# Router stages rank nodes by running counts and two matmuls per group; biases of the node and output layers are added by VectorE

## The chip, the cores and the metric
One core of a Trainium2 chip. The metric is the device time of one execution of the whole program, in microseconds (us): 5182.44 us before, the median of three runs (5175.28 to 5185.94).

## The reference, cut to what matters
A graph of 6250 nodes with 256 features and 106,250 edges goes through two layers, and every part adds to x:

```
x += gcn(layernorm(x))        # relu(A @ (h W1) + b1), then A @ (h W2) + b2
x += moe(layernorm(x))        # 6 experts, top 2 by a small router network
x += gnn(layernorm(x))        # x1 = mish(h Wd + bd); agg = sum relu(x1[src] + mish(edge We + be))
                              # out = mish((x1 + agg) Wo + bo)
x += moe(layernorm(x))        # 8 experts, top 2 by a linear router
```
mish(z) = z tanh(softplus(z)). The biases that the change touches are b2 (of the first part), bd (dense) and bo (out). All arithmetic is float32.

## The kernel before, in words
Nodes stand in tiles of 128 (a node per partition) and are worked on in groups of up to four tiles (UNITS: twelve groups of four tiles and a last one of one tile). x stays in SBUF for the whole program. Stages run one after the other, each with its own buffers and semaphores, and between two of them stands a barrier of all engines. Within a stage the order of the work on each engine is written out by hand; there is no planner. Every `chain(...)` and `link(...)` on VectorE waits for the instruction just issued.

The stages in order: setup; support (h W1, lines 302 to 378); convolution over the edges; hidden; convolution again; router 0 with the dispatch to its experts (stage_dispatch, mix 0); experts 0; nodes (stage_nodes: the weighted outputs of the experts are added to x, then x1); edges; router 1 (stage_dispatch, mix 1); experts 1; the last additions. The change touches support, router 0, nodes and router 1.

Support, a loop over 13 groups in halves of two tiles. VectorE: normalise (line 281) four tiles, copy (342) two halves from PSUM; ScalarE copies transposes; TensorE transposes and multiplies; SyncE stores rows. VectorE does the normalisation of group g+1 before the copies of group g.

Router stages, for group u. TensorE: turned (transposes, 931), hidden (1357, router 0 only), ranks (1380 to 1384) of the group before, logits (1365 or 1370), product (1341, then 1342 for the bias) of a later group: two ahead in router 0, three ahead in router 1, which has two PSUM buffers for it. Product waits until VectorE has taken the earlier product (`moments_ready`). The bias is the sum of three bf16 rows, multiplied by ones of three partitions; `split_bias` (866 to 873) makes these rows by ten linked VectorE instructions at the start of the stage, behind which `parts_ready` releases TensorE and ScalarE. VectorE: added (1487, or 1491 and 1492), moments (897, 900), biased (1503), chose (1514 to 1529: the two best experts of a node as a mask `chosen`), refined (913 to 917), rows_of (1536 to 1545: the row to which a node goes for each of its two experts), bounded (1480, router 1 only: min(z, 20), the start of mish). ScalarE: evacuated, factor (the four activations of mish, router 1), guessed, spread (923: the normalised nodes), rectified (1434, router 0). GpSimd scatters the nodes to the experts' rows, two indirect DMAs for each tile, when `row_ready` says so.

In ranks each node gets the number of nodes ahead of it that chose the same expert: one matmul of the strict upper triangle `before` by `chosen`, one of all ones by the tiles 1, 2 and 3 back (three matmuls of 24, 16 and 8 columns), and four of all ones for the group's total.

Nodes stage, for group u. VectorE: combined(u+1) (998 and the moments), finished(u-1) (1019), refined(u+1), bounded(u) (1011). ScalarE: evacuated, factor(u-1), guessed and spread of u+1, keep(u-2). TensorE: turned(u), turned_back(u-2), product(u) (1104, with 1105 for the bias). GpSimd gathers the experts' outputs.

Of the kernel before, what the change touches and what calls it, by code (L numbers as in the profile page):

```python
# [9 lines left out]
ALU = mybir.AluOpType  # L10
# [3 lines left out]
P = 128  # L14
# [6 lines left out]
TG = 4  # L21
# [279 lines left out]
def stage_support(nc, c):  # L301

    io = c.io
    with ExitStack() as ctx:
# [7 lines left out]
        rows = [sb(f"s_rows{h}", [P, 2, HID]) for h in range(2)]  # L312
        ps_t = [pb(f"s_pt{h}", [P, KD, 2 * P]) for h in range(2)]
        ps_y = [pb(f"s_py{h}", [P, 2, HID]) for h in range(2)]
        w_in, own = sem("s_w_in"), sem("s_own")
# [6 lines left out]
        @block.sync  # L322
        def _(sp):
            sp.dma_start(w1[:], io["g_w1"]).then_inc(w_in, 16)
            with sp.Fori(0, G) as g:
                for h in range(2):
                    store_rows(sp, c.t1, g, h, rows, rows_ready, rows_out)

            for h in range(2):
                sp.wait_ge(rows_out[h], 16)  # L330

        @block.vector
        def _(dve):
# [3 lines left out]
            def copy_rows():  # L337
                for h in range(2):
# [5 lines left out]
                    dve.sem_inc(rows_ready[h], 1)  # L344

            for h in range(2):
                dve.sem_inc(py_free[h], 1)
                normalise(dve, nc, c, xn[h], 0, h, xn_ready[h])
            with dve.Fori(0, G - 1) as g:
# [4 lines left out]
                copy_rows()  # L354
            copy_rows()
# [579 lines left out]
def stage_nodes(nc, c):  # L935
# [5 lines left out]
    with ExitStack() as ctx:  # L941
# [5 lines left out]
        bias, parts, ones = bias_buffers(sb)  # L947
# [6 lines left out]
        w_in, parts_ready, own, act_own, parts_own = sem("w_in"), sem("parts_ready"), sem("own"), sem("act_own"), sem("parts_own")  # L954
# [22 lines left out]
        def _(sp):  # L977
            sp.dma_start(wd[:], io["l_wd"]).then_inc(w_in, 16)
            sp.dma_start(bias[0][:], io["l_bd"]).then_inc(w_in, 16)
# [8 lines left out]
        def _(dve):  # L988
# [33 lines left out]
            nc.vector.memset(ln2[:], LN2)  # L1022
            nc.vector.memset(ones[:], 1.0)
# [17 lines left out]
        def _(act):  # L1041
# [31 lines left out]
            act.wait_ge(parts_ready, 1)  # L1073
# [17 lines left out]
        def _(pe):  # L1091
# [6 lines left out]
            def product(u):  # L1098
# [3 lines left out]
                for s in range(UNITS[u][1]):  # L1102
                    for k in range(KD):
                        pe.matmul(ps_y[u % 2][:, s, :], xt[:, k, s * P:(s + 1) * P], wd[:, k, :], start=k == 0, stop=False)
                    last = pe.matmul(ps_y[u % 2][:, s, :], ones[:], parts[:], start=False, stop=True)
# [8 lines left out]
            pe.wait_ge(parts_ready, 1)  # L1114
# [137 lines left out]
def stage_dispatch(nc, c, mix):  # L1252
# [8 lines left out]
    with ExitStack() as ctx:  # L1261
# [4 lines left out]
        bias, parts, ones3 = bias_buffers(sb)  # L1266
        if mix == 0:
# [3 lines left out]
            loads = [(wx[:, 0, :], "g_w2"), (bias[0][:], "g_b2"), (w1[:], "r0_w1"), (b1[:], "r0_b1"), (w2[:], "r0_w2")]  # L1271
        else:
            wx = sb("wx", [P, KD, D])
            gamma, beta, w2 = sb("gamma", [P, KD]), sb("beta", [P, KD]), sb("w2", [P, KD, E1])
            q, ln2 = pair(sb, "q", [P, TG, D]), sb("ln2", [P, 1])
            loads = [(wx[:], "l_wo"), (bias[0][:], "l_bo"), (gamma[:], "r1_gamma"), (beta[:], "r1_beta"), (w2[:], "r1_w2")]
# [8 lines left out]
        is_nth, chosen = sb("is_nth", [P, 2, NT, 8]), pair(sb, "chosen", [P, TG, 8])  # L1285
        first, running = sb("first", [P, 8]), pair(sb, "running", [P, 8])
# [12 lines left out]
        w_in, parts_ready = sem("w_in"), sem("parts_ready")  # L1299
        own, act_own, parts_own = sem("own"), sem("act_own"), sem("parts_own")  # L1300
# [4 lines left out]
        logit_ready, exp_ready, chosen_ready = sem("logit_ready"), sem("exp_ready"), sem("chosen_ready")  # L1305
# [28 lines left out]
        def _(pe):  # L1334
            def product(u):
# [3 lines left out]
                for s in range(n):  # L1339
                    for k in range(mix + 1):  # L1340
                        pe.matmul(ps_x[u % X][:, s, :], c.feat[:, k, (t + s) * P:(t + s + 1) * P], wx[:, k, :], start=k == 0, stop=False)
                    last = pe.matmul(ps_x[u % X][:, s, :], ones3[:], parts[:], start=False, stop=True)
# [30 lines left out]
            def ranks(u):  # L1373
                n = UNITS[u][1]
                flat = lambda ap: ap.rearrange("p t e -> p (t e)")
                now = chosen[u % 2]
                pe.wait_ge(chosen_ready, u + 1)
# [328 lines left out]
```

## Time and profile before

| | |
|---|---|
| median of three runs | 5182.44 us |
| the profiled execution's own time | 5180.41 us |
| its span | 5178.6 us |
| TensorE busy | 3895.7 us (75%) |
| VectorE busy | 1965.5 us (38%) |
| ScalarE busy | 1566.8 us (30%) |
| GpSimd busy | 2875.4 us (56%) |

The share of busy time is a mean over stages with different limits. The four stages of the change fill about 690 us of the span: support from 73 to 129 us, router 0 from 2398 to 2642, nodes from 3019 to 3187, router 1 from 4313 to 4540. The row "PEclk" of the page gives the clock that was granted to TensorE, in tenths of 2.4 GHz: 9 in support, 5 to 6 in the slices of router 0 and of router 1, 7 to 9 in the other stages.

### The profile page before, as it was taken

The page shows a single profiled execution, that of the slowest core. Times are in us where ns is not written, and L with a number is a line of the kernel's source. Part 1 is how long each engine was busy: PE and PEld are TensorE (multiplying, and loading weights), DVE is VectorE, ACT ScalarE, POOL GpSimd, SP SyncE. Part 2 cuts the span into 40 slices and gives each one's busy share as a digit, 9 for nine tenths or more (in the row PEclk, how much of TensorE's full clock was granted, in tenths as well). Part 3 has the DMA queues.
Part 4 walks back from the last instruction along what each step waited for, and adds up shares of the span by engine and source line. Part 5 has one row for each costly group of instructions (what it writes and reads, how often), then busy time and mean ns, then how long its engine had stood idle before and what let it go on. Part 6 is the DMA issues. An engine that isn't in the chain of part 4 may idle for free. (4 is left out here: it accounts for less than half of the span.)

```text
span 5178.6 us, 61257 instructions
## 1 busy us (share of the span) xinstructions
PE 3895.7 (75%) x16707; PEld 3012.1 (58%) x16707; DVE 1965.5 (38%) x4145; ACT 1566.8 (30%) x1876; POOL 2875.4 (56%) x2950
## 2 busy tenths in 40 slices
PE   3688888885788898896959966666666667769980
PEld 2455555553556565564548755666666665558870
DVE  4344344433344444433423354333333334511113
ACT  1344444443344444443201145212122123411110
POOL 0677777772777777772420055777777772600007
PEclk9778788876787778776579976555555556689995
DMA  3455555554454554552132234666666662242214
GB/s 95 140 175 171 166 173 173 177 169 116 125 156 150 157 157 150 155 156 69 66 130 85 81 113 133 197 200 197 201 199 199 200 198 61 82 154 65 65 61 144
DMA packets 336091, 733.21 MB, mean 142 GB/s; under 512 B 67797, under 2 KB 184672, under 8 KB 335897
## 3 DMA queue, kind: packets, MB, share of 16 engines
q1 hardware_dynamic: 160968, 392.16, 21.9%
q0 software_dynamic: 118176, 284.72, 20.1%
q10 hardware_dynamic: 56880, 55.58, 3.2%
q8 instruction: 25, 0.41, 0.0%
q14 instruction: 42, 0.34, 0.0%
HBM read 521.27 MB, written 210.91 MB: 141 GB/s over the span
## 5 line engine op out<-in xcount | busy, mean ns | idle before, releaser
L582 PE MATMUL conv_pz<-conv_we,conv_edge 128*128 128x256 f32 x3360 | 1221.0, 498 | 0.0
L1188 PE MATMUL x_pa<-x_hot,x_node 128*128 128x64 f32 x3360 | 765.7, 423 | 359.6 <-PEq L72 359.6
L464 POOL DMA_INDIRECT conv_gath<-support_table,conv_idx x840 | 808.0, 962 | 404.1 <-issue 249.8
L1173 POOL DMA_INDIRECT x_node<-node_table,x_idx x840 | 852.3, 1015 | 297.2 <-issue 234.9
L464 POOL DMA_INDIRECT conv_gath<-hidden_table,conv_idx x840 | 808.8, 963 | 346.7 <-issue 247.4
L1188 PEld LDWEIGHTS x_pa<-x_hot,x_node 128*128 128x128 f32 x3360 | 732.5, 331 | 393.0 <-issue 393.0
L582 PEld LDWEIGHTS conv_pz<-conv_we,conv_edge 128*128 128x128 f32 x3360 | 729.3, 241 | 181.7 <-issue 49.5
L573 PE MATMUL conv_ps<-conv_hot,conv_gath 128*128 128x64 f32 x3360 | 524.5, 311 | 358.9 <-DMA conv_gath<-support_table,conv_idx 187.7
L573 PEld LDWEIGHTS conv_ps<-conv_hot,conv_gath 128*128 128x128 f32 x3360 | 474.0, 221 | 404.5 <-DMA conv_gath<-support_table,conv_idx 197.3
L883 ACT ACTIVATE conv_q<-conv_q 128x1024 f32<-128x1024 f32 x210 | 221.9, 1057 | 1201.2 <-ACTq L72 1176.9
L1209 DVE TENSOR_TENSOR x_node<-x_node,x_neg 128x1024 f32<-128x1024 f32 x210 | 257.4, 1226 | 626.4 <-DMA x_node<-node_table,x_idx 626.4
L1198 ACT ACTIVATE x_node<-x_node 128x1024 f32<-128x1024 f32 x210 | 221.9, 1057 | 899.2 <-ACTq L72 899.2
L474 DVE TENSOR_SCALAR conv_q<-conv_pz 128x1024 f32<-128x1024 f32 x210 | 257.2, 1225 | 608.8 <-DVEq L72 606.9
L675 POOL DMA_INDIRECT cb_outs<-expert_outs,row x98 | 96.0, 980 | 523.1 <-PEq L658 493.6
L782 PE MATMUL e_ph<-e_xt,e_w_first 128*128 128x256 f32 x1376 | 313.6, 385 | 61.6 <-PEq L72 61.6
L1326 POOL DMA_INDIRECT expert_rows<-r_xn,r_row x196 | 196.8, 1004 | 291.3 <-DVE r_row L1545 238.3
L821 ACT ACTIVATE e_hid<-e_ph,e_b_first 128x256 f32<-128x256 f32 x344 | 137.8, 473 | 710.4 <-ACTq L72 710.4
L490 DVE TENSOR_TENSOR sums_table<-sums_table,conv_ps 128x64 f32 x420 | 93.3, 222 | 618.0 <-DVEq L72 615.5
L782 PEld LDWEIGHTS e_ph<-e_xt,e_w_first 128*128 128x128 f32 x1376 | 259.7, 192 | 106.1 <-issue 73.1
L971 POOL DMA_INDIRECT n_outs<-expert_outs,row x98 | 95.1, 970 | 400.6 <-POOLq L97 367.4
L583 PEld LDWEIGHTS conv_pz<-conv_bias_parts,conv_ones 3*128 3x128 bf16 x840 | 77.8, 93 | 365.0 <-issue 365.0
L583 PE MATMUL conv_pz<-conv_bias_parts,conv_ones 3*128 3x256 bf16 x840 | 258.8, 308 | 0.0
(221 smaller groups left out, 4234.4 us busy)
## 6 DMA issues: line engine op xcount, KB each, us to landing
conv_edge<-in_edge_t SPq DMA_DIRECT2D x210, 512.0 KB, 5.0
edge_mish_table<-conv_neg SPq DMA_DIRECT2D x210, 512.0 KB, 3.1
x_neg<-edge_mish_table SPq DMA_DIRECT2D x210, 512.0 KB, 3.5
e_rows<-expert_rows SPq DMA_DIRECT2D x114, 256.0 KB, 3.0
expert_outs<-e_outs ACTq DMA_DIRECT2D x114, 256.0 KB, 2.2
expert_outs<-conv_zeros ACTq DMA_DIRECT2D x35, 512.0 KB
conv_gath<-support_table,conv_idx POOLq DMA_INDIRECT x840
conv_gath<-hidden_table,conv_idx POOLq DMA_INDIRECT x840
```

Of the source, the lines that this page charges most:

```text
L464: pool.indirect_dma_start(gath[s][:, j, :], None, table[:, :], bass.IndirectOffsetOnAxis(ap=idx[:, half, col:col + 1], axis=0),).then_inc( ...
L474: nc.vector.tensor_scalar(q[r][:], ps_z[r][:], ZMAX, None, ALU.min).then_inc(z_ready[r], 1)
L573: last = pe.matmul(ps[s % 2][:], gath[s][:, j, :], hot[half][:, at + j, :], start=j == 0, stop=j == CG - 1)
L582: pe.matmul(ps_z[r][:, j, :], edge[r][:, m, j * P:(j + 1) * P], we[:, m, :], start=m == 0, stop=False)
L583: last = pe.matmul(ps_z[r][:, j, :], ones[:], parts[:], start=False, stop=True)
L782: last = pe.matmul(out[:, m, :], w[:, k, m * P:(m + 1) * P], given[:, k, :], start=k == 0, stop=k == KD - 1)
L883: link(act, act.activation(q, q, ACT.Exp), own)
L1173: pool.indirect_dma_start(node[s][:, j, :], None, c.t3[:, :], bass.IndirectOffsetOnAxis(ap=idx[:, half, col:col + 1], axis=0),).then_inc(g ...
L1188: last = pe.matmul(ps_a[n][:, m, :], node[s][:, j, m * P:(m + 1) * P], hot[n][:, j, :], start=j == 0, stop=j == CG - 1)
L1198: act.activation(node[s][:], node[s][:], ACT.Relu, scale=-1.0).then_inc(msg_ready, 1)
L1209: nc.vector.tensor_tensor(node[s][:], node[s][:], neg[s % RING][:], ALU.add).then_inc(own, 1)
L1326: pool.indirect_dma_start(c.rows_d[:, :], bass.IndirectOffsetOnAxis(ap=row[0:rows, t + s, k:k + 1], axis=0), xn[u % RING][0:rows, s, :], None,
```

## The change
1. Routers: `split_bias`, its buffers and its semaphore go. The constants are made ahead of the wait for the loads, with `consts_ready` in place of `parts_ready`.
2. Router 0: product no longer adds b2; the load of b2 leaves this stage.
3. Support: b2 is loaded for all partitions, VectorE waits for it before its first instruction, and after each copy it adds b2 to the two tiles of x that have been normalised.
4. Nodes and router 1: the bias is loaded for all 128 partitions; product has no matmul for it; bounded first adds it to the product in PSUM (128x1024 elements), waits, and then takes the minimum.
5. Routers, ranks: VectorE multiplies `chosen` by a table of ones and zeros (`upto`) and sums, which gives for each tile the count of the tiles ahead of it in the group and, as a fifth, the total. TensorE then needs two matmuls: ones by these sums (40 columns) and `before` by `chosen` (32 columns), into the same PSUM. The convolution stages keep their three bf16 rows.

```diff
@@ support, VectorE
                     dve.sem_inc(rows_ready[h], 1)
+                    half = c.x[:, bass.ds(g * TG + 2 * h, 2), :]
+                    nc.vector.tensor_tensor(half, half, b2[:].unsqueeze(1).to_broadcast([P, 2, D]), ALU.add)
+            dve.wait_ge(b_in, 16)
             for h in range(2):
@@ nodes, bounded (router 1 has the same with ps_x)
                 dve.wait_ge(py_ready, u + 1)
+                chain(nc.vector.tensor_tensor(ps_y[u % 2][:, 0:n, :], ps_y[u % 2][:, 0:n, :], bias[:].unsqueeze(1).to_broadcast([P, n, D]), ALU.add))
                 nc.vector.tensor_scalar(q[u % 2][:, 0:n, :], ps_y[u % 2][:, 0:n, :], ZMAX, None, ALU.min).then_inc(z_ready, 1)
@@ nodes and routers, start of VectorE's work
             dve.wait_ge(w_in, 32)
-            split_bias(dve, nc, c, bias, parts, parts_own)
-            dve.sem_inc(parts_ready, 2)
@@ routers, product on TensorE
                     for k in range(mix + 1):
-                        pe.matmul(ps_x[u % X][:, s, :], c.feat[...], wx[:, k, :], start=k == 0, stop=False)
-                    last = pe.matmul(ps_x[u % X][:, s, :], ones3[:], parts[:], start=False, stop=True)
+                        last = pe.matmul(ps_x[u % X][:, s, :], c.feat[...], wx[:, k, :], start=k == 0, stop=k == mix)
@@ routers, ranks on TensorE
-                pe.matmul(flat(ps_r[:, 0:n, :]), before[:], flat(now[:, 0:n, :]), start=True, stop=n == 1)
-                for d in range(1, n):
-                    pe.matmul(flat(ps_r[:, d:n, :]), ones[:], flat(now[:, 0:n - d, :]), start=False, stop=d == n - 1)
-                for s in range(n):
-                    last = pe.matmul(ps_r[:, TG, :], ones[:], now[:, s, :], start=s == 0, stop=s == n - 1)
-                last.then_inc(rank_ready, 1)
+                pe.matmul(flat(ps_r[:, 0:n + 1, :]), ones[:], flat(sums[u % 2][:, 0:n + 1, :]), start=True, stop=False)
+                pe.matmul(flat(ps_r[:, 0:n, :]), before[:], flat(chosen[u % 2][:, 0:n, :]), start=False, stop=True).then_inc(rank_ready, 1)
@@ routers, end of chose on VectorE
-                last.then_inc(chosen_ready, 1)
+                chain(last)
+                slots = upto[:, 0:n + 1, :, 0:n]
+                taken = now.rearrange("p s e -> p e s").unsqueeze(1).to_broadcast([P, n + 1, 8, n])
+                chain(nc.vector.tensor_tensor(counted[:, 0:n + 1, :, 0:n], taken, slots, ALU.mult))
+                nc.vector.tensor_reduce(sums[u % 2][:, 0:n + 1, :], counted[:, 0:n + 1, :, 0:n], AX.X, ALU.add).then_inc(sums_ready, 1)
```

## Rows read from the trace of the kernel before

**Rows 1.** Busy time by engine, granted clock and DMA in steady stretches of both routers
```profile
2434.00:2582.00 148.00, 137.32 (x440) 83.58 (x439) 62.76 (x360) 39.46 (x81) 65.29 (x68) 0.56 0.17 60
4377.00:4480.00 103.00, 95.59 (x464) 69.83 (x464) 68.04 (x297) 62.01 (x90) 62.40 (x59) 0.75 0.22 77
```
**Rows 2.** Timeline, router 0's start: start us, us, engine, line [idle before, its releaser]
```profile
2404.17 0.28 DVE L866 CAST r_bias_high<-r_bias 3x256 bf16<-3x256 f32 x1 [5.09 <-DMA r_before<-in_before]
...
2409.46 1.19 PE L1341 MATMUL r_px<-r_wx,sums_table 128*128 128x256 f32 x2 [22.66 <-DVEq L1555]
...
2410.59 0.39 PE L1342 MATMUL r_px<-r_bias_parts,r_ones 3*128 3x256 bf16 x1
...
2410.91 1.22 PE L1341 MATMUL r_px<-r_wx,sums_table 128*128 128x256 f32 x2
```
**Rows 3.** Timeline, router 0's loop
```profile
2437.86 1.22 DVE L1487 TENSOR_TENSOR x_sb<-x_sb,r_px 128x1024 f32<-128x1024 f32 x1 [4.15 <-PE r_px L1342]
...
2487.54 1.22 DVE L1487 TENSOR_TENSOR x_sb<-x_sb,r_px 128x1024 f32<-128x1024 f32 x1 [5.18 <-PE r_px L1342]
...
2505.03 1.22 DVE L1487 TENSOR_TENSOR x_sb<-x_sb,r_px 128x1024 f32<-128x1024 f32 x1 [5.18 <-PE r_px L1342]
...
2519.53 1.22 DVE L1487 TENSOR_TENSOR x_sb<-x_sb,r_px 128x1024 f32<-128x1024 f32 x1 [3.80 <-PE r_px L1342]
...
2582.49 1.22 DVE L1487 TENSOR_TENSOR x_sb<-x_sb,r_px 128x1024 f32<-128x1024 f32 x1 [5.18 <-PE r_px L1342]
...
2588.04 0.16 DVE L917 SCALAR_TENSOR_TENSOR r_shift<-mv,rstd 128x4 f32<-128x4 f32 x1
...
2590.93 1.66 PE L1365 MATMUL r_pl<-r_w,r_hid 128*128 128x6 f32 x8 [1.60 <-ACT r_hid L1434]
```
**Rows 4.** Timeline, router 0's last but one ranks
```profile
2606.76 0.63 PE L1380 MATMUL r_pr<-r_chosen,r_before 128*128 128x32 f32 x2 [0.37 <-DVE r_chosen L1526]
...
2608.49 1.85 PE L1384 MATMUL r_pr<-r_chosen,r_ones 128*128 128x8 f32 x8
```
**Rows 5.** Lines 1543 and 1608: ns min/median/max, first and last start us, forms
```profile
L1543 DVE TENSOR_REDUCE r_row_f<-r_picked x52: 151/178/187, 2447.0 to 4512.9; 128x4 f32<-128x32 f32 x48, 128x1 f32<-128x8 f32 x4
...
L1608 DVE TENSOR_TENSOR r_picked<-r_is_nth,r_start_f x4: 558/562/569, 2620.1 to 4517.0; 128x392 f32<-128x392 f32 x4
```
**Rows 6.** Timeline, support's loop on VectorE
```profile
104.76 0.42 DVE L342 COPY s_rows<-s_py 128x256 f32<-128x256 f32 x1 [0.55 <-DVEq L72]
...
106.21 1.39 DVE L281 TENSOR_SCALAR s_xn<-x_sb,mv,rstd 128x256 f32 x4 [1.02 <-DVEq L72]
```
**Rows 7.** Line 281: VectorE's register instructions for an address in x
```profile
L281 DVEq FUSED_REGOPS  x96: 65/84/117, 77.4 to 121.9; - x96
```
**Rows 8.** Line 859: a VectorE add of two tiles
```profile
L859 DVE TENSOR_TENSOR e_outs<-e_py,e_b_last x114: 691/691/693, 2677.0 to 5036.9; 128x512 f32<-128x512 f32 x114
```
**Rows 9.** Timeline, support's start
```profile
73.71 0.36 SPq L324 DMA_DIRECT2D gw<-in_g_w  x1
74.46 1.38 DVE L281 TENSOR_SCALAR s_xn<-x_sb,mv,rstd 128x256 f32<-128x256 f32 x4 [1.41 <-PEq L97]
...
76.07 1.94 PE L290 MATMUL s_pt<-ident_sb,s_xn 128*128 128x128 f32 x8 [76.07 <-PEq L72]
```
**Rows 10.** Timeline, router 1's loop
```profile
4432.73 1.23 DVE L1480 TENSOR_SCALAR r_q<-r_px 128x1024 f32<-128x1024 f32 x1 [3.53 <-PE r_px L1342]
...
4438.26 2.08 PE L1341 MATMUL r_px<-r_wx,messages_table 128*128 128x256 f32 x4 [1.04 <-DVE mv L900]
...
4446.40 1.22 DVE L1480 TENSOR_SCALAR r_q<-r_px 128x1024 f32<-128x1024 f32 x1 [3.53 <-PE r_px L1342]
...
4481.06 0.96 POOL L1326 DMA_INDIRECT expert_rows<-r_xn,r_row  x1 [2.91 <-DVE r_row L1545]
```
**Rows 11.** Timeline, nodes' first combined and the finished with the least idle before it
```profile
3031.58 3.38 DVE L998 SCALAR_TENSOR_TENSOR x_sb<-n_outs,gate,x_sb 128x256 f32<-128x256 f32 x8 [4.18 <-DMA n_outs<-expert_outs,row]
...
3115.19 1.22 DVE L1019 SCALAR_TENSOR_TENSOR n_rows<-n_q,n_py 128x1024 f32<-128x1024 f32 x1 [1.83 <-ACT n_q L1066]
```

More of the change, by code:

```diff
@@ L946, in stage_nodes @@
         wd = sb("wd", [P, KD, D])
-        bias, parts, ones = bias_buffers(sb)
+        bias = sb("bias", [P, D])
         ln2 = sb("ln2", [P, 1])
@@ L978, in _ @@
             sp.dma_start(wd[:], io["l_wd"]).then_inc(w_in, 16)
-            sp.dma_start(bias[0][:], io["l_bd"]).then_inc(w_in, 16)
+            sp.dma_start(bias[:], io["l_bd"]).then_inc(w_in, 16)
             for u, (t, n) in enumerate(UNITS):
@@ L1103, in product @@
                     for k in range(KD):
-                        pe.matmul(ps_y[u % 2][:, s, :], xt[:, k, s * P:(s + 1) * P], wd[:, k, :], start=k == 0, stop=False)
-                    last = pe.matmul(ps_y[u % 2][:, s, :], ones[:], parts[:], start=False, stop=True)
+                        last = pe.matmul(ps_y[u % 2][:, s, :], xt[:, k, s * P:(s + 1) * P], wd[:, k, :], start=k == 0, stop=k == KD - 1)
                 last.then_inc(py_ready, 1)
@@ L1270, in stage_dispatch @@
             hid = sb("hid", [P, GN])
-            loads = [(wx[:, 0, :], "g_w2"), (bias[0][:], "g_b2"), (w1[:], "r0_w1"), (b1[:], "r0_b1"), (w2[:], "r0_w2")]
+            loads = [(wx[:, 0, :], "g_w2"), (w1[:], "r0_w1"), (b1[:], "r0_b1"), (w2[:], "r0_w2")]
         else:
@@ L1340, in product @@
                     for k in range(mix + 1):
-                        pe.matmul(ps_x[u % X][:, s, :], c.feat[:, k, (t + s) * P:(t + s + 1) * P], wx[:, k, :], start=k == 0, stop=False)
-                    last = pe.matmul(ps_x[u % X][:, s, :], ones3[:], parts[:], start=False, stop=True)
+                        last = pe.matmul(ps_x[u % X][:, s, :], c.feat[:, k, (t + s) * P:(t + s + 1) * P], wx[:, k, :], start=k == 0, stop=k == mix)
                 last.then_inc(px_ready, 1)
@@ L1478, in bounded @@
                 n = UNITS[u][1]
+                got = ps_x[u % X][:, 0:n, :]
                 dve.wait_ge(px_ready, u + 1)
+                chain(nc.vector.tensor_tensor(got, got, bias[:].unsqueeze(1).to_broadcast([P, n, D]), ALU.add))
                 nc.vector.tensor_scalar(q[u % 2][:, 0:n, :], ps_x[u % X][:, 0:n, :], ZMAX, None, ALU.min).then_inc(z_ready, 1)
@@ L1548, in _ @@
                 nc.vector.memset(logit[r][:], -1e30)
-            nc.vector.memset(ones[:], 1.0)
-            nc.vector.memset(ones3[:], 1.0)
+            chain(nc.vector.memset(upto[:], 0.0))
+            for s in range(1, TG + 1):
+                nc.vector.memset(upto[:, s, :, 0:s], 1.0)
             if mix == 1:
                 nc.vector.memset(ln2[:], LN2)
+            nc.vector.memset(ones[:], 1.0).then_inc(consts_ready, 1)
             dve.wait_ge(w_in, 16 * len(loads))
-            split_bias(dve, nc, c, bias, parts, parts_own)
-            dve.sem_inc(parts_ready, 2)
             nc.vector.tensor_scalar(first[:], iota8[:], float(REGION), None, ALU.mult)
@@ L1697 @@
         "g_w2": a["L0_gnn_W2"],
-        "g_b2": np.broadcast_to(a["L0_gnn_b2"], (3, D)),
+        "g_b2": np.broadcast_to(a["L0_gnn_b2"], (P, D)),
     }
```

44 lines of the change are left out of this document (22 added, 22 removed).

## The prediction
> **What bounds the kernel now.** The shares of the page say little here: the change touches four stages of twelve, so I read each of them by itself. In each, the first view is the timeline around its first instructions (what releases the stage), the second the timeline of two or three rounds of its loop (which wait comes back each time), the third the busy times with the granted clock.
>
> Router 0: at its start VectorE has waited for the last load and then runs the ten linked instructions of the split, and TensorE's first product waits behind them, from 2404.17 to 2409.46 [rows 2]. In its loop every VectorE addition (line 1487) waits for the product, 4 to 5 us each time [rows 3], and TensorE is busy 137 of 148 us at 0.56 of full clock [rows 1]: TensorE closes the round. But a second chain is nearly as long: from the addition over VectorE's moments, chose and refined, ScalarE's spread and rectified, to the logits. Where TensorE is a little ahead, it waits for that chain: 1.60 us before the logits at 2590.93 [rows 3].
>
> Router 1: one serial round of 13.67 us (4432.73 to 4446.40): VectorE's bounded, added and moments take 5.5 us to the start of the product at 4438.26, the product 8.1 us to the next bounded [rows 10]. GpSimd, which ends the stage, still waits for rows at 4481.06 (idle 2.91) [rows 10] and hardly afterwards.
>
> Support: VectorE's own queue is the round. Nothing else is waited for; the gaps of 0.55 and 1.02 us are its semaphore and register instructions [rows 6]. Nodes: ScalarE and TensorE close the round; VectorE has at least 1.83 us of idle before finished, but for the first group [rows 11].
>
> **The change, part by part.** Minus is a gain.
>
> *Router 0.* (a) Start: the split goes, 2409.46 - 2404.17 = 5.3 us, all of it ahead of TensorE; the load of b2 goes too, one DMA issue on SyncE ahead of the last load, by the 0.36 us of one issue [rows 9]. Together -5.6. What is late next is the last load itself. (b) Product: from the bias matmul to the next tile are 2410.91 - 2410.59 = 0.32 us, and a tile takes 2410.91 - 2409.46 = 1.45 [rows 2]. Four tiles save 1.28 us at this clock (1.2 GHz). Three rounds at the start have no ranks in them: -3.8. (c) The loop proper: nine rounds from 2437.86 to 2582.49, 144.6 us; a slow one is 17.49 (2487.54 to 2505.03), a fast one 14.50 (to 2519.53) [rows 3]. Ranks at half clock take 2606.76 to 2608.49 + 1.85 = 3.6 us for 16 record pairs of ones and `before` [rows 4]; two matmuls (four pairs) leave about a quarter, 0.9 to 1.1. So TensorE's chain shortens by 1.3 + 2.6 us in a slow round and the other chain closes it. That one grows: chose gets two instructions and two waits. Their price lies between 0.18 us (32 elements) and 0.56 (392 elements) [rows 5]; for 160 elements I take 0.30 each, nearer the lower row, plus the overlap lost to the waits: 0.66 in all (ends 0.4 and 1.2). The new slow round: addition to refined 2588.04 - 2582.49 = 5.55, plus 0.66, then 2.89 to the logits (2590.93), 1.5 logits, product 4 x (1.45 - 0.32) = 4.5, 0.1 to the addition: 15.2 to 15.3 us. The fast round, with logits of 0.9 and part of the product at full clock, comes to 14.1 to 14.2. Of the nine rounds four are slow, one is between: 4 x 2.2 + 1 + 4 x 0.4 = -11 (ends: all slow -7, all fast -17). (d) The last round, with a product of one tile, is closed by the other chain already: +0.35. The last ranks that GpSimd waits for come 1.3 sooner. Router 0: -5.6 - 3.8 - 11 + 0.35 - 1.3 = **-21.4** (-17 to -27). GpSimd has idle before nearly every group, so it isn't late next.
>
> *Support.* The extra instruction is an addition of two tiles; the nearest row is 0.69 us [rows 8], and its address needs one or two register instructions of 0.08 each (some 0.12 apart) [rows 7]. VectorE's queue runs ahead of the engine, so some of it lies beside the semaphore instructions. Between the two copies stand five of them in 0.55 us, 0.11 each [rows 6]: three come before the addition, two beside it. The second copy comes at 0.33 + 0.25 + 0.69 - 0.08 = 1.19 instead of 0.55: +0.63. The second addition starts 0.58 after its copy and ends at 1.27; the loop's own instructions behind it (0.7 to 0.8 of the 1.02) reach the next normalisation at 1.35: +0.33. Per group +0.95; twelve loop rounds and one first half at the end: +12.0. The very last addition lies beside the store. VectorE's new wait at the start: the load before it is usable 76.07 - 73.71 = 2.36 us after its issue, the new one one issue later, so the first normalisation moves from 74.46 to about 76.4; TensorE did nothing before 76.07 anyway and starts at 77.2 to 77.4 [rows 9]: +1.3, and what is queued behind that wait is the whole of VectorE's work. Support: **+13.3** (+3 if only the register instructions show, +26 with all 26 additions, 0.94 each, in full and 1.9 at the start).
>
> *Nodes.* Start: the split lies beside the first gather, for which VectorE still waits 4.18 us [rows 11]: 0. Loop: bounded gets an addition of 128x1024, 1.22 us as line 1487 [rows 3], and its wait: +1.24 a group on VectorE. Behind it are combined and finished; finished has 1.83 us of cover at the least [rows 11], so 0.6 remains and the round stays; the product's gain is hidden too, since bounded starts behind refined. The first group has no cover, but its product ends 1.3 us sooner. In the last two groups ScalarE stands close behind bounded: +0.75 and +0.45. Nodes: **+1.2** (0 to +8).
>
> *Router 1.* Start as in router 0, without the missing load: -5.2; the load of the bias is now 128 rows, within 0.2. The round: +1.24 for the addition, which nothing covers, as product waits for the moments; the product loses four bias matmuls, three at 0.32 and one, at full clock, some 0.2: -1.17. Net +0.08, ten rounds +0.8. chose and the shorter ranks lie in VectorE's 3.5 us of idle and in TensorE's 1.04 [rows 10]: 0. The rows of the group at 4481.06 come behind one more addition: +1.24. Router 1: **-3.2** (-9 to +7, by the clock of the product).
>
> A rule of the Trainium skill speaks against this part ("TensorE: Matmul & The Clock Gate", the Part on the clock gate): TensorE's default is the throttled clock, and activity releases it. Work is taken from TensorE here, so by it the product could stay at 1.2 GHz.
>
> **Sum.** -21.4 + 13.3 + 1.2 - 3.2 = -10.1 us. The profiled execution took 5180.41 us (span 5178.6), 2.0 below the median of the three runs, so 5170.3 by the profile and 5172.3 beside the median. I say **5172**.
>
> **The rivals.** (1) The clock falls. The row for it: in router 0 the clock is at 0.56 although TensorE is busy 93% [rows 1], so it is low with little idle already, and idle comes on top. Against it: router 1, busy 93% as well, has 0.75 [rows 1], so the busy share alone doesn't set it. Price: router 1's product wholly at 1.2 GHz is 4 x 2.0 = 8.0, with 6.8 of VectorE 14.9 instead of 13.67, +12 over ten rounds; router 0 all slow +4: 5188. By the page's rule this is where it would go. (2) VectorE's additions cost less and router 0's rounds all take 14.2: -6 more there, and -6 in support, if the additions lie beside more of its queue: 5160. For it: every slow round of before has the long ranks in it. (3) The slower side: the addition is exposed wherever it stands. It decides in nodes: once finished's cover of 1.83 is used up (a turn of TensorE at full clock shortens the round by some 0.7), each of 13 groups costs 1.24, +15 over my sum, and support +12.7 more, at the full 0.94: 5200. Against it: most groups have 2 to 3 us there. (4) The routers' starts don't gain, since something else releases TensorE there: +10, 5182. Against it: the release is named as line 1555, right behind the split [rows 2].
>
> **How the numbers follow.** 0.2% of this kernel, 10.4 us, is about what a measurement can tell from no change. The forecast 0.50, of which half lies beyond -10.4 (own range 5163 to 5181); rival 1 0.13; rival 2 0.22; rival 3 0.07; rival 4 0.05; something else 0.03. Faster by over 0.2%: 0.25 + 0.22 + 0.02 = 0.49; within: 0.25 + 0.13 + 0.05 + 0.01 = 0.44; slower: 0.07. The range leaves out rival 3 and the far ends of support's and router 0's bounds: 5157 to 5187.
>
> **What would show it.** Router 0's first product about 0.1 us behind the last load's landing; line 1487 coming every 14.1 to 15.3 us, TensorE waiting for r_hid before line 1365 in every round; support's rounds 0.95 us longer, the second copy 1.2 us behind the first instead of 0.55; line 1480 still every 13.6 to 13.8 us in router 1 with about 6.8 us from the bias addition to the product; nodes unchanged within 2 us. I am wrong if support's round grows by less than 0.5 or over 1.3 us, if router 1's round moves by more than 0.5, or if router 0 as a whole gains less than 15 us.

## The result, and the profile after

| | before | after |
|---|---|---|
| median of five runs each | 5175.87 us (5175.28 to 5185.94) | 5153.29 us (5151.17 to 5159.08) |
| ratio, 95% interval | | 0.9953 (0.9939 to 0.9968) |
| span of the profiled execution | 5178.6 us | 5151.5 us |

The kernel is 0.47% faster, by more than the 0.2% that a measurement can tell. Forecast were 5172 us and -10.1 us. Stage by stage, each from its first instruction to the next stage's first, in us:

| | before | after | measured | forecast |
|---|---|---|---|---|
| support | 56.15 | 64.79 | +8.6 | +13.3 |
| hidden (not touched) | 42.14 | 43.65 | +1.5 | 0 |
| router 0 | 243.81 | 219.29 | -24.5 | -21.4 |
| nodes | 167.82 | 169.72 | +1.9 | +1.2 |
| router 1 | 226.67 | 216.53 | -10.1 | -3.2 |
| the other stages | | | -4.5 | 0 |

The stages add up to the difference of the two profiled spans, 27.1 us; the medians differ by 22.6. Of the profiles used further down, those of c2, e3, e5 and e11 are of executions over 1.5% slower than the fastest of their kernel.

The busy times by engine in both routers' loops after, as in [rows 1]: the columns are the stretch, its length, busy us of PE, PEld, DVE, ACT and POOL, granted clock, DMA share and GB/s.
```profile
2434.47:2566.42 131.95, 84.01 (x290) 61.54 (x289) 67.47 (x379) 39.47 (x81) 66.25 (x70) 0.73 0.19 68
4324.34:4443.14 118.80, 85.75 (x394) 72.47 (x393) 95.75 (x380) 74.11 (x108) 61.72 (x60) 0.76 0.19 66
```
TensorE's clock in router 0 has risen from 0.56 [rows 1] to 0.73, though TensorE is now busy only 84 of 132 us. I had set out the opposite as a rival. In router 1 it is 0.76, against 0.73 in the nine rounds of before (4348.89 to 4473.71).

The mean hides where the clock rose. Two stretches of one round of router 0 after, same columns: hidden, then the logits with the product.
```profile
2481.21:2483.19 1.98, 1.98 (x4) 0.67 (x4) 1.81 (x21) 0.50 (x2) 0.84 (x1) 1.00 0.37 132
2487.76:2493.04 5.28, 5.28 (x17) 4.46 (x17) 0.55 (x3) 0.22 (x1) 3.98 (x5) 0.50 0.30 104
```
Hidden had 0.50 in the same place of a slow round before (2490.50 to 2494.28). Over the loops its records fell from 1088 to 618 ns on average, while those of the logits, which come behind a wait, rose from 309 to 361 ns, and nearly every product has 0.50.

Timeline after, router 0: the start, and one round of the loop (for [rows 2, 3]).
```profile
2411.02 3.78 PE L1343 MATMUL r_px<-r_wx,sums_table 128*128 128x256 f32 x8 [16.94 <-DMA r_before<-in_before]
...
2478.58 1.22 DVE L1485 TENSOR_TENSOR x_sb<-x_sb,r_px 128x1024 f32<-128x1024 f32 x1 [3.00 <-PE r_px L1343]
...
2483.39 0.42 DVE L1531 TENSOR_TENSOR r_counted<-r_chosen,r_upto 128x160 f32<-128x160 f32 x1
2483.84 0.32 DVE L1532 TENSOR_REDUCE r_sums<-r_counted 128x40 f32<-128x160 f32 x1
...
2484.86 0.16 DVE L922 SCALAR_TENSOR_TENSOR r_shift<-mv,rstd 128x4 f32<-128x4 f32 x1
...
2487.76 1.87 PE L1366 MATMUL r_pl<-r_w,r_hid 128*128 128x6 f32 x8 [2.91 <-ACT r_hid L1430]
2489.49 3.76 PE L1343 MATMUL r_px<-r_wx,sums_table 128*128 128x256 f32 x8
...
2493.28 1.22 DVE L1485 TENSOR_TENSOR x_sb<-x_sb,r_px 128x1024 f32<-128x1024 f32 x1 [3.00 <-PE r_px L1343]
```
The product now waits for the last load itself. (Each matmul stands in the trace as records: two for one in f32, one in bf16.) In the loop TensorE waits for r_hid each round, and the round is 14.70 us: 6.28 to L922, 2.90 to the logits, 1.73, and 3.79 for the product. Each of the nine rounds takes 14.4 to 14.7 us.

Router 1 before, where my price for the bias matmul came out wrong: two tiles of the product that begins at 4438.26 [rows 10].
```profile
4440.26 0.39 PE L1342 MATMUL r_px<-r_bias_parts,r_ones 3*128 3x256 bf16 x1
...
4440.58 2.08 PE L1341 MATMUL r_px<-r_wx,messages_table 128*128 128x256 f32 x4
...
4442.59 0.39 PE L1342 MATMUL r_px<-r_bias_parts,r_ones 3*128 3x256 bf16 x1
...
4442.91 1.97 PE L1341 MATMUL r_px<-r_wx,messages_table 128*128 128x256 f32 x4
```
Router 1 after, one round:
```profile
4416.16 1.23 DVE L1477 TENSOR_TENSOR r_px<-r_px,r_bias 128x1024 f32<-128x1024 f32 x1 [1.76 <-PE r_px L1343]
4417.43 1.22 DVE L1478 TENSOR_SCALAR r_q<-r_px 128x1024 f32<-128x1024 f32 x1
...
4422.95 6.61 PE L1343 MATMUL r_px<-r_wx,messages_table 128*128 128x256 f32 x16 [2.46 <-DVE mv L905]
...
4429.60 1.23 DVE L1477 TENSOR_TENSOR r_px<-r_px,r_bias 128x1024 f32<-128x1024 f32 x1 [1.97 <-PE r_px L1343]
```
A tile with its bias took 4442.91 - 4440.58 = 2.33 us at 1.2 GHz. With no bias between them the records stand 0.427 apart at that clock (start times of the single records), so a tile of four without bias is 1.71, and the bias costs 0.62, not 0.32. Of the 0.62, 0.21 is a record half as long as the others; 0.14 passes before it starts and the rest behind it. Router 1's round is 13.44 here, 6.79 of it VectorE and 6.65 the product (8.14 before). Tile by tile this product lost 0.45, 0.62, 0.41 and 0.10 us: before, the clock went to full 6.38 us into it, ahead of the last tile; after, 5.88 us into it, in the middle of the last tile. The shorter product gets less of the full clock, 0.54 on average for 0.60.

Support after, one round on VectorE (for [rows 6]):
```profile
87.18 0.42 DVE L344 COPY s_rows<-s_py 128x256 f32<-128x256 f32 x1
88.04 0.69 DVE L348 TENSOR_TENSOR x_sb<-x_sb,s_b 128x512 f32 x1 [0.44 <-DVEq L72]
88.65 0.42 DVE L344 COPY s_rows<-s_py 128x256 f32<-128x256 f32 x1
89.51 0.69 DVE L348 TENSOR_TENSOR x_sb<-x_sb,s_b 128x512 f32 x1 [0.44 <-DVEq L72]
90.24 1.40 DVE L281 TENSOR_SCALAR s_xn<-x_sb,mv,rstd 128x256 f32 x4
91.55 0.42 DVE L344 COPY s_rows<-s_py 128x256 f32<-128x256 f32 x1
```

### The profile page after: what moved, and what is told of

Read it like the earlier page. It is cut to its first block and busy times, and to the rows that moved or that the text cites. A ratio compares the mean times of both kernels' runs of the same rounds, so it can differ in the third digit from the quotient of the medians.

```text
span 5151.5 us, 60460 instructions
## 1 busy us (share of the span) xinstructions
PE 3786.7 (74%) x16272; PEld 2974.7 (58%) x16272; DVE 2015.3 (39%) x4226; ACT 1568.8 (30%) x1876; POOL 2872.9 (56%) x2950
```

## The experiments

Six of these sixteen runs were timed where the convolutions take their 1115 us (e7 to e10, e15, e16). The other ten were made on three chips whose gathers are slower (e1 to e4, then e5 and e6, then e11 to e14): a convolution takes 1520 to 1650 us there and either kernel 6250 to 6480, so a whole time tells nothing of a change of 20 us. There I compare stages, with both kernels profiled once more (c1 and c2, on the chip of e5 and e6). Support agrees with the first profiles within 0.4 us, router 0 is 6 to 7 us longer and router 1 6 to 8, and one kernel's stage can differ by 5 us from profile to profile. Times are us; "round" is from one addition or minimum to the next.

| stage | before there (c1) | after there (c2) |
|---|---|---|
| support, hidden | 56.14, 42.15 | 64.44, 43.67 |
| router 0 | 250.75 | 225.19 |
| nodes | 199.40 | 207.44 |
| router 1 | 233.10 | 224.48 |

**Ranks alone, and biases alone.** Theory: the gain that I missed is the bias matmul. Rival: it is the ranks, by way of the clock. e1 is the kernel before with part 5 of the change, e2 the changed kernel without it:
```diff
-                pe.matmul(... ones[:], sums ...)     # e1 adds these two to before,
-                pe.matmul(... before[:], chosen ...) # e2 takes them from after
+                pe.matmul(flat(ps_r[:, 0:n, :]), before[:], flat(now[:, 0:n, :]), start=True, stop=n == 1)
...
+                for s in range(n):
+                    last = pe.matmul(ps_r[:, TG, :], ones[:], now[:, s, :], start=s == 0, stop=s == n - 1)
```


> The kernel before with the counts by VectorE and the two matmuls for ranks alone; all biases as before. Theory (the gain that I missed is the bias matmul, which costs 0.62 us a tile at 1.2 GHz, not the 0.32 that I took): in router 0 VectorE's chain closes the rounds at once, since the product still takes 4 x 1.47 = 5.9 us: 6.3 from the addition to refined, 2.9 to the logits, 1.6, 5.9, 0.1, so slow rounds of 16.8 instead of 17.49, fast ones as before, last ranks 1.5 sooner: router 0 -3 to -6 us; router 1's rounds stay at 13.67 us, TensorE only waits longer for the moments. In all -3 to -7 us. Rival (the short ranks let TensorE's clock rise, and that is what made both routers faster): router 0 gains 15 us or more with rounds of 14.7, router 1 gains 5 or more, in all -20.

> The changed kernel with the old ranks (up to eight matmuls per group, no counts by VectorE). Theory: router 1 stays as in the changed kernel (216.5 us, rounds of 13.2 to 13.6); in router 0 TensorE closes the slow rounds again, 17.49 - 4 x 0.62 = 15.0 us, the fast ones are 14.1, and the last ranks come 1.5 us later: router 0 some 219 to 223 us. In all 0 to +5 us to the changed kernel. Rival (ranks and clock): router 1 goes back to rounds of at least 14.3 us (13.67 + 1.24 - 4 x 0.15 or more) and router 0 to 230 us or more, in all +15 or more.

e1: router 0 251.06 (c1: 250.75; -3 to -6 was expected), its rounds mostly 16.9 as worked out; router 1's rounds 13.65 to 13.84, the stage 232.23. The ranks alone give nothing that shows: the chain with the product in it closes the rounds, at about the mean of what c1 has, 14.8 to 17.7. e2: router 0 222.49, router 1 219.84. The biases alone give all of it, within the 5 us between profiles. A second run of e2:

> The changed kernel with the old ranks once more, as the first run of it was on a chip with slow gathers. It tells what the counts and the two matmuls give in router 0 beside the biases. By rows of the changed kernel: TensorE's chain with the old ranks is 17.49 - 4 x 0.62 = 15.0 us in slow rounds, 14.0 in fast ones, against 14.7 by VectorE's chain with the counts; last ranks 1.8 us later. Router 0 219 to 223, in all 0 to +4 us to the changed kernel. Rival (the ranks carry most of router 0's gain): router 0 at 228 or more.

226.44 and 224.59, against 225.19 and 224.48 of the changed kernel in c2. By the two runs, the two matmuls and the counts that they need change router 0 by -1.3 and +2.7 us, on three different chips: no effect that can be told from nothing. The rival, a gain of 15 us by the ranks, is out.

**The price of the bias matmul: left out, twice, in other forms.** e3 leaves `pe.matmul(..., ones3[:], parts[:], ...)` out of the kernel before in nodes and routers, e4 issues it twice in the routers.

> The kernel before without the bias matmul of product in both routers and in nodes, and nothing in its place, so these biases are left out; the split is still made. It prices the bias matmul by itself. Theory (0.62 us a tile at 1.2 GHz, 0.40 at 2.4): router 1's product takes 6.0 to 6.7 us instead of 8.1 and its round 11.4 to 12.1 instead of 13.67, ten rounds -16 to -22; router 0's slow rounds fall by 2.4 to 15.0, the stage -12 to -18; nodes within 2 us. In all -28 to -40. Rival (0.32 a tile, as I predicted): router 1's round 12.5, -12, router 0 -8 to -10, in all -20.

> The kernel before with each bias matmul of the two routers issued twice (the bias counts twice there). It tells where the 0.62 us sit. Theory: most of it is what stands between an f32 matmul and the bf16 one, ahead of it (0.57 instead of 0.43 to its start) and behind it (0.59 instead of 0.43 in the next tile's first), so a second one right behind the first adds only about 0.2 us (half of the 0.43 between two f32 matmuls of as many columns) at 1.2 GHz: router 1's round 13.67 + 0.6 to 0.8 = 14.3 to 14.5, in all +12 to +18 over both routers. Rival (each three-row matmul costs its 0.62 wherever it stands): router 1's round 15.7 to 16.1, in all +45 or more.

e3: router 1's undisturbed rounds took 10.96 to 12.33 us, behind a first of 12.94; two of its twelve took 19 and 21, with idle time on VectorE that the profile puts down to no instruction of the kernel (2.59 us ahead of one logits addition), so the stage (227.36) hides the gain. Router 0 took 228.71, nodes 199.99. The eight undisturbed ones are 11.5 on average, 2.2 less than 13.67 or 0.54 a tile, at a clock between the two levels; 0.32 a tile would have left 12.4. e4: ten rounds of 14.66 on average (four of 13.2 to 13.4, six of 15.4 to 15.9, by the clock of the product), +1.0, for four more bias matmuls, 0.25 each. So the price sits around the first and not in the matmul:
```profile
5504.87 0.39 PE L1342 MATMUL r_px<-r_bias_parts,r_ones 3*128 3x256 bf16 x1
5505.06 0.42 PE L1343 MATMUL r_px<-r_bias_parts,r_ones 3*128 3x256 bf16 x1
5505.41 1.53 PE L1341 MATMUL r_px<-r_wx,messages_table 128*128 128x256 f32 x3
```
The second starts 0.19 behind the first. What makes the stall, the change of type or the change to 3 rows? e9 and e12 change the kernel before:
```diff
-  last = pe.matmul(ps_x[u % X][:, s, :], ones3[:], parts[:], start=False, stop=True)
+  last = pe.matmul(ps_x[u % X][:, s, :], ones[0:1, :], bias[0][0:1, :], start=False, stop=True)   # e9: f32, 1 row
+  last = pe.matmul(ps_x[u % X][:, s, :], ones_b[:], parts_b[:], start=False, stop=True)           # e12: bf16, 128 rows
```


> The kernel before with the bias in product as one f32 row times one f32 row of ones, instead of three bf16 rows. It tells whether the 0.4 us around the bias matmul come with the change of type. If they do, nothing stands around it and it costs its two records of 0.43: router 1's tile is 6 x 0.427 = 2.56 us at 1.2 GHz (2.33 with bf16) and its round some 14.2 to 14.6. If they come with the change from 128 rows to few, they stay: tile 2.9 to 3.0 and round 15 to 15.5. For router 0's clock: if the change of type holds it down, it rises to about 0.73 here; if more work between the waits holds it down, it stays at 0.5 to 0.6.

> The kernel before with the bias matmul of the routers on 128 bf16 rows (the three parts and 125 rows of zeros, by ones) instead of 3. It tells whether the stall around the bias matmul and the low clock come from the few rows or from the type. Rows: no stall, the tile is 1.71 + 0.21 = 1.9 us at 1.2 GHz (2.33 with 3 rows), router 1's round 12.0 to 12.6 instead of 13.67, and router 0's clock 0.68 to 0.75. Type: tile 2.3 and round 13.7 as before, clock of router 0 0.56 to 0.62.

Timeline of TensorE in router 1's product, first e9 (f32, one row), then e12 (bf16, 128 rows):
```profile
4599.11 2.05 PE L1341 MATMUL r_px<-r_wx,messages_table 128*128 128x256 f32 x4
4601.10 1.22 PE L1342 MATMUL r_px<-r_bias,r_ones 1*128 1x256 f32 x2
4602.24 1.22 PE L1341 MATMUL r_px<-r_wx,messages_table 128*128 128x256 f32 x2
```
```profile
5609.92 1.91 PE L1342 MATMUL r_px<-r_wx,messages_table 128*128 128x256 f32 x4
5611.63 0.42 PE L1343 MATMUL r_px<-r_parts_b,r_ones_b 128*128 128x256 bf16 x1
5611.84 1.85 PE L1342 MATMUL r_px<-r_wx,messages_table 128*128 128x256 f32 x4
```
With 128 rows nothing is lost: 1.71 us for the four records, 0.21 for the bias, 1.92 a tile. With one f32 row the tile is 3.14, of which 1.43 for the bias where two full records would be 0.85. So the few rows cause the stall, the type doesn't. The expected rounds of 15 to 15.5 us for e9 were far off, though: they took 21.04, because the clock stayed at 0.50 (below). Nor did e12's shorter rounds of router 1 show in the stage: nine of the twelve took 11.4 to 13.3 us, but two took 21, with VectorE idle as in e3, and the stage 233.43, as in c1. Its router 0 took 236.08, 15 less than in c1. In router 1 the gain by wide rows shows in e15 alone. The Trainium skill ("TensorEngine Tiling (Array Packing)", section Tiling Modes) says that changing the tiling mode drains TensorE. I read 3 rows beside 128 as such a change, which the page doesn't say. The traces agree with this reading: the stall is 0.41 us around the first 3-row matmul, none around a second (e4), 0.58 with one row (e9) and 0 with 128 rows (e12).

**Starts.** e8 puts one conversion in place of the ten instructions of the split.

> The kernel before with one conversion in place of the ten linked instructions of the split, so the bias rows are wrong (each holds the whole bias); product is as before. It prices the starts alone. Theory: the first product of each router comes 4.6 to 4.9 us sooner (nine tenths of 5.3), nothing else moves: router 0 and router 1 some -4.8 each, nodes 0. Rival (another release takes its place, the starts don't gain): within 1 us of before in each router. The bias matmul stays as it is, so the clock of router 0's loop stays at 0.55 to 0.62.

From the stage's start to the first product: router 0 6.11 us instead of 10.85, router 1 6.05 instead of 10.64, -4.7 and -4.6. As worked out; rival 4 is out. Router 0 as a whole took 235.58, its rounds 14.5 to 17.5 at a clock of 0.61: so much do these rounds vary by themselves (250.75 and 243.81 in the two profiles of before).

**VectorE's additions.** e5 leaves the three out of the changed kernel, e6 adds b2 elsewhere:
```diff
                 if mix == 0:
+                    chain(nc.vector.tensor_tensor(x, x, bias[:].unsqueeze(1).to_broadcast([P, n, D]), ALU.add))  # e6
                     dve.wait_ge(px_ready, u + 1)
```


> The kernel before, unchanged, once more, because the four runs before this took 1540 to 1620 us in each convolution instead of 1115, and a profile of before under the same conditions is wanted for the clock. Theory (the bias matmul between products keeps TensorE's clock low in router 0; the ranks do not): router 0's loop has a mean granted clock of 0.55 to 0.60, and the stage takes 243 to 258 us. Rival (the ranks-only kernel was slow there because short ranks let the clock fall): the rounds have at least three of 14.5 us and the stage takes 244 or less, where ranks alone took 251.

> The changed kernel, unchanged, once more beside the kernel before. All theories: support 64.8 us, router 0 219 and router 1 216.5, as these hardly depend on how fast the gathers are; the sum of the four stages some 24 us under before. Theory: clock 0.73 in router 0's loop.

> The changed kernel without VectorE's additions of b2 (support), bd (nodes) and bo (router 1), so these biases are left out; loads and waits stay. It prices the additions by stage. Theory: support's rounds go back from 4.38 to 3.72 us, 12 x 0.66 = -7.9, and the 1.9 of the start stay: 56.8 us; nodes -1 to -2; router 1's chain is VectorE then the product, so the round falls by all 1.25: 12.0 to 12.3, or less if the GpSimd queue closes it, stage -9 to -13. Rival (in router 1 the addition is half hidden, since the product is waited for anyway): router 1 -6 or less. Rival in support (the additions lie beside the register instructions and the time went at the start): support still over 60.

> The changed kernel with b2 added in router 0 instead of support: VectorE adds it to x of the group ahead of its wait for the product, where it is idle for 2.7 to 3.0 us. Support has no load, wait or addition. Theory: support back to 56.2 (-8.6), router 0 unchanged but for one load more (+0.4) and nothing in the loop, as 1.25 is less than the idle time: 219 to 220; -8 us to the changed kernel. Rival (the addition delays what stands behind it, the round grows): router 0 +6 or more, nothing gained.

c1 and c2 are the table above; router 0's clock was 0.61 in c1 and 0.72 in c2. Router 1's 224.48 is 8 over the 216.5 expected of both, its rounds the same, the rest in its last stretch. e5: support 57.64, so 6.8 us are additions and 1.5 the new wait; nodes 198.97, the 8 us more of the changed kernel on this chip gone; router 1's first rounds 10.9 to 12.7, later ones up to 16.1 (stage 217.40). e6: support 55.19 and router 0 222.33: b2 is free in router 0's wait. Hidden takes 43.64 to 43.89 in every run with additions in support and 42.13 to 42.18 without them, although nothing of it was changed. It looks like a second price of part 3, but e15 and e16, which have no additions there, took 42.9; I did not test the cause.

**What the clock follows.** e10 has TensorE compute hidden a second time, into a PSUM buffer that nobody reads, in its wait for r_hid; e13 does it from one of the 128 rows.
```diff
                 last.then_inc(ph_ready, 1)
+                for k in range(KD):
+                    pe.matmul(ps_f[:, 0:n * P], w1[:, k, :], xt[u % 2][:, k, 0:n * P], ...)              # e10
+                    pe.matmul(ps_f[:, 0:n * P], w1[0:1, k, :], xt[u % 2][0:1, k, 0:n * P], ...)          # e13
```


> The changed kernel with four more matmul records per group in router 0: hidden is computed a second time into a PSUM buffer that nobody reads, in TensorE's wait for r_hid (1.5 and 2.9 us idle per round), so the path hardly changes. It tells what made the clock of router 0's loop rise from 0.56 to 0.73. Theory A (TensorE's waits did: more f32 work in the gaps takes them away): the clock falls to 0.65 or less, and the rounds grow from 14.7 to 15.5 or more. Theory B (the bf16 matmuls between f32 ones held it down): the clock stays at 0.72 to 0.74 and the round within 0.3 us.

> The changed kernel with the same filler in router 0 as the run that computed hidden twice, but from one row of the 128: the same count and columns of matmul records, nearly nothing of the array in use. It tells what the clock follows. If it follows how much of the array works: the clock doesn't rise above 0.73, rounds stay at 14.7 or grow to 15.5, the stage 219 to 226. If it follows how much of the time TensorE is busy in the profile: 0.86 and 207 us, as with 128 rows.

Router 0's loop, same columns as above: e10, e13, e12, e1, and last router 1's loop in e9.
```profile
2428.50:2549.50 121.00, 87.11 (x328) 59.87 (x326) 68.44 (x379) 39.47 (x81) 64.35 (x67) 0.86 0.20 72
```
```profile
3477.00:3615.00 138.00, 101.47 (x331) 68.75 (x330) 68.23 (x379) 39.46 (x81) 66.45 (x70) 0.73 0.18 65
```
```profile
3405.00:3542.00 137.00, 99.08 (x430) 72.88 (x430) 61.81 (x360) 39.47 (x81) 64.50 (x68) 0.76 0.18 64
```
```profile
3368.00:3519.00 151.00, 119.67 (x326) 66.97 (x326) 68.19 (x379) 39.46 (x81) 67.20 (x71) 0.58 0.17 60
```
```profile
4486.00:4654.00 168.00, 168.00 (x512) 120.62 (x511) 70.50 (x321) 64.96 (x96) 61.62 (x64) 0.50 0.14 51
```
Both theories on e10 were wrong. More matmuls in the gaps raised the clock from 0.73 to 0.86, and router 0 fell from 219.29 to 207.11 us; here the product gains as well, its records took 541 ns instead of 646. The same number of records from one row left the clock at 0.73 (rounds 15.2 to 15.7, stage 228.13, against 0.72 and 225.19 in c2). With the bias on 128 rows and nothing else changed it was 0.76 (e12). Short ranks did nothing to it (e1, 0.58). And a TensorE that is busy without a gap, with a one-row matmul in each tile, had 0.50 throughout (e9: router 1 309.11 us, rounds of 21.04; its edges stage took 57 us more as well, for which I have no cause). So the busy share doesn't set the clock: full-height matmuls in the wait raised it, those of one row did not.

The rule of the Trainium skill that I weighed in the prediction ("TensorE: Matmul & The Clock Gate", the Part on the clock gate) is that activity releases the throttle. The traces agree for full-height matmuls (e10, 0.86) and not for those of one row (e13, 0.73); the page doesn't tell the two apart. A stage that nothing touched sets a limit to the height as well. The edges stage before:
```profile
3300.00:4200.00 900.00, 623.22 (x2737) 596.23 (x2736) 333.56 (x570) 180.67 (x171) 691.92 (x684) 0.50 0.63 199
```
All of TensorE's matmuls there have 128 rows (and 64 columns), it is busy 623 of 900 us, and it was granted 0.50 all through (so "7 to 9 in the other stages", above, leaves this stage out). Height alone doesn't account for the clock either, and what does stays open.

**Versions.** e7 is e6 with two waits shortened, e11 adds the filler:
```diff
-                    pe.wait_ge(moments_ready, u - X + 1)
+                    pe.wait_ge(px_free, u - X + 1)       # signalled right behind the last read of that PSUM buffer
...
                 if u and mix == 0:
+                    counts(u - 1)                        # behind refined(u + 1), was the end of chose(u - 1)
                     rows_of(u - 1)
```


> A version meant to beat both: b2 in router 0's wait as in the run before, and two waits shortened. In router 1 product waits until VectorE has read the PSUM buffer for the last time (the line that multiplies by it), not for the moments 3.1 us later. In router 0 the counts stand behind refined instead of ahead of it. Theory: router 1's round is VectorE up to the product plus the product, so it falls by what TensorE then waits no more, 2.4 us, from 13.43 to 11.0 to 11.5 (VectorE is busy 11.1 us a round): stage -18 to -24. Router 0's round loses the 0.75 us of the counts: 14.0 instead of 14.7, stage -5 to -7. In all -30 to -38 to the changed kernel. Rival (GpSimd's scatters, 10.2 us a round with 2.9 idle, become the bound): router 1 -5 to -10 only, with GpSimd never idle.

> The version with the two shortened waits, and in router 0 the second hidden into an unread PSUM buffer as well, since that filler took router 0 from 219.3 to 207.1 us at a clock of 0.86. Theory (full matmuls in the waits raise the clock, and the product and logits run at it): router 0's rounds 12.0 to 13.6 instead of 14.2, stage 200 to 205 instead of 211; the rest as in that version. In all 5107 to 5113 us. Rival (with the counts behind refined the chain is VectorE's and ScalarE's, and the filler only delays ranks): within 2 us of 5118.6.

e7: 5118.55 us, ratio to before 0.9896 (0.9837 to 0.9955). Router 1 200.44 with rounds of 11.5 to 12.3, router 0 211.25 with rounds of 14.2, support 55.80. e11 was timed on a chip with slower gathers: router 0 214.06 at 0.84, 11 less than in c2. But router 1 took 224.19 there, as in c2, with rounds of up to 17.75: what the early release gave in e7 didn't show. Its whole time tells nothing.

e15 is the kernel before with nothing changed but the height of every bias matmul, e16 is e11 with that in the convolutions:
```diff
-            sb("bias_parts", [3, D], BF16), sb("ones3", [3, P], BF16))
+            sb("bias_parts", [P, D], BF16), sb("ones3", [P, P], BF16))   # parts set to zero first, rows 0 to 2 as before
```


> The kernel before with every bias matmul (convolutions, nodes, both routers) on 128 bf16 rows, of which 125 are zeros, in place of 3; nothing else changed, no addition moved to VectorE. It sets the other cure beside the change's. If the few rows are the whole cost: router 1's round 11.4 to 12.5 us (stage -12 to -16), router 0 -8 to -15 with a clock of 0.70 to 0.76, and in the convolutions TensorE's busy time falls by about 0.35 us for each of 840 bias matmuls, 300 us; of that only what is not waited away for gathers shows (97.7 of 700 us are such waits), between 0 and -60 us for both. In all -25 to -85 to before. Rival (the convolutions are bound by the gathers): they stay within 3 us each and the whole gains 20 to 30.

> The version with two shortened waits, b2 in router 0's wait and the filler, and with the bias matmuls of the convolutions on 128 rows. Theory: the gains add, since the stages are apart: router 0 200 to 205 us and router 1 200 on an undisturbed chip, convolutions as in the run with wide rows everywhere. In all 5110 us less what the convolutions gain. Rival (the filler gives nothing beside the moved counts): router 0 stays at 211.

e15: 5120.67 us, ratio 0.9904 (0.9887 to 0.9920). Router 0 216.74 with the old ranks, router 1 208.33 with rounds of 11.4 and 12.6, convolutions 1106.68 and 1104.20. Router 0's loop:
```profile
2420.00:2543.40 123.40, 92.25 (x436) 66.67 (x433) 61.90 (x361) 39.48 (x81) 65.22 (x68) 0.82 0.20 72
```
So 125 rows of zeros do more than the whole change (0.9904 against 0.9953), without its 26 additions in support. Router 0 gained 27 us, where 8 to 15 were expected, at a clock of 0.82 for the expected 0.70 to 0.76. In the convolutions TensorE's saved time went into waits for gathers (176.8 us of them from 500 to 1200, 95.2 before), and 16 us came through, where I had expected up to 60. e16: 5098.73 us, ratio 0.9862 (0.9846 to 0.9879), with router 0 at 201.76 and router 1 at 199.85, as low as in any run. Its convolutions took 1112.76 and 1104.26, so of the 16 us of e15 it has 10.

## Why the prediction was wrong

- **The failed step is (b), "from the bias matmul to the next tile are 0.32 us".** It prices the record and not what it does to its neighbours: I didn't set two tiles with and without it side by side. The cost is 0.62 us at 1.2 GHz, and at full clock 1.27 - 0.87 = 0.40 (the last tile of the same product, 4445.02 to 4446.29, against four records 0.216 apart). Three tiles at the lower clock and one at the higher make 2.26 a round, where I had 1.17. By that and 1.24 for the addition, nine rounds of router 1 would have lost 9.2 us; they lost 6.0, where I had +0.8 for ten, since the shorter product gets less of the full clock (13.87 to 13.20 us on average, rounds of 11.9 to 13.6). This makes up the miss of router 1, -10.1 for -3.2, and one of my signs of being wrong came with it: its round moved by more than 0.5. In router 0 the product takes 3.79 in a slow round instead of 4.5.
- **Rival 1, the clock falls: refuted for the loops, in part true for the product.** I read the clock by how busy TensorE is. The mean of both loops rose, in router 0 from 0.56 to 0.73, and removing the few-row matmuls alone does that (e3, e12). But the rise lies in hidden, in the transposes and in waits. Behind the wait for r_hid the logits and the product run at 0.50, and in router 1 the product fell from 0.60 to 0.54, as the rival had it; at the right price of the bias that cost some 3 us and not 12.
- **Rival 2, the fastest one at 5160, lay nearest, and for another reason.** Router 0's rounds all became short, though of 14.4 to 14.7 us and not 14.2, and support came out 4.7 below the sum. But its evidence, that every slow round of before has the long ranks in it, misled: e2 and e14 have the long ranks, and at most 15.8 us.
- **Router 0's chain was right.** The three first rounds gave -5.0 us (-3.8), the nine -12.7 (-11). Addition to refined 6.28 (6.21 forecast), to the logits 2.90 (2.89), last round +0.6 (+0.35), end -1.8 (-1.3), start -5.7 (-5.6). The pair in chose cost 0.42 + 0.32 (0.30 each). But it credited the ranks with the gain in slow rounds. e1 and e2 show that the product's own saving of 2.3 us (5.88 to 3.55, from its first record to the next transpose) does that alone: it shortens both chains, the ranks only TensorE's. (The ranks of before are 16 records, eight pairs, where I wrote 16 pairs; the quarter that is left is right.)
- **Starts: right** (-5.7, -5.1; e8).
- **Support: right mechanism, term too large.** The round grew by 0.65 (4.37 for 3.72), not 0.95. The second copy came 1.05 us behind the end of the first, where 0.55 had been and 1.19 was forecast: +0.50. The next normalisation came 1.17 behind the end of the second copy, where 1.03 had been and 1.35 was forecast: +0.14. The copy stands directly behind the addition, without idle time, so VectorE's queue works off its semaphore instructions during the addition, more of them than I had taken. The start cost 1.5 (e5 against c1) to 1.8 us (first transpose 4.19 behind the stage's first instruction, 2.36 before); 1.3 was forecast.
- **Nodes: right in size on the first chip** (+1.9 for +1.2): finished still has 1.84 us of idle before it in most groups (0.84 at the least), but all rounds now take 11.1 to 11.8, where three took 10.7 to 11.0. On the chip with slow gathers rival 3 came half true, +8.0.
- The forecast was also set beside a median of 5182.44; that of five runs is 5175.87, 6.6 of the 19 us of error. Beside it the same sum gives 5166 and the same width 5151 to 5181, which holds 5153.29, with step (b) as wrong as it is. Another 4.5 us lie in stages that nothing touched, where one profile of each kernel tells little.

## What to carry to other kernels

Price an instruction on TensorE by the spacing of its neighbours with it and without it, not by its own row. A bias, or any small accumulation between full matmuls, is best given all 128 rows, with zeros in the unused ones: here that is worth more than moving it to VectorE. Work that is moved goes where its engine waits, as b2 in router 0, not into a loop that its engine closes.

## What the runs showed of the hardware that was not expected

- A 3-row bf16 matmul between 128-row f32 ones (256 columns) costs 0.62 us at 1.2 GHz and 0.40 at 2.4; at 1.2 GHz a second one starts 0.19 behind it, on 128 rows it costs 0.21, and one f32 row costs 1.43.
- TensorE busy in every microsecond of 168 had a clock of 0.50 (e9), and busy 87 of 121 one of 0.86 (e10). Matmuls whose result nobody reads made a stage 12 us shorter.
- A higher mean clock of a loop says nothing of the stretch that matters: router 0's rose from 0.56 to 0.73 while nearly all its products and logits ran at 0.50.
- An untouched stage (hidden) took 1.5 us more in every kernel with the additions in support, and 0.8 more in two others (e15, e16).
